# A perceiver layer with experts: the end of the delta-rule stage rewritten to run tile by tile, with the router moved into it

## The reference, cut to what matters

```python
h = rmsnorm(layernorm(x, ln1_g, ln1_b), rms_in_w)
q, k, v = conv_silu(h @ Wq), conv_silu(h @ Wk), conv_silu(h @ Wv)    # 4 heads, keys of 64, values of 128
q, k = l2norm(q) * 64 ** -0.5, l2norm(k)
g, beta = -exp(A_log) * softplus(h @ Wa + dt_bias), sigmoid(h @ Wb)
o = gated_delta_rule(q, k, v, g, beta)                               # a recurrence over the 64 tokens
o = rmsnorm(o, o_norm_w) * silu(h @ Wg)
x1 = xl + o @ Wo
x = x + x1 + gelu(layernorm(x1, ln2_g, ln2_b) @ W2 + b2)
# the experts
n = layernorm(x)
logits = n @ Wr + br                                                 # 8 experts
y = x + softmax(logits)[top] * (gelu(n @ W1[top] + b1[top]) @ W2[top] + b2[top])
```

## Time and profile before

| | us |
|---|---|
| median of 3 runs | 843.79 |
| lowest, highest | 839.43, 844.43 |
| profiled execution, its own time | 846.05 |
| its span in the trace | 844.3 |

### The profile page before, as it was taken

How to read it: one execution, slowest core, us unless ns; L and a number is a source line. 1 busy time by engine, 2 the same in 40 slices (tenths; PEclk the granted TensorE clock), 3 DMA queues, 4 the chain that set the end, 5 groups by cost and what they waited for, 6 DMA issues and landing times. The chain is left out here.

```text
span 844.3 us, 18960 instructions
## 1 busy us (share of the span) xinstructions
PE 684.7 (81%) x7638; PEld 525.9 (62%) x7638; DVE 421.2 (50%) x907; ACT 328.4 (39%) x881; POOL 144.2 (17%) x213
## 2 busy tenths in 40 slices
PE   3778887789899999995787689989986764278996
PEld 2556665565456666663665546579985643178995
DVE  5436787764545445514587275836657344011111
ACT  1235444443445544442577363331224141132332
POOL 1011112201100000003334232091000211211121
PEclk9879998999999999995889699989998965598999
DMA  6920000001900000004000000000000009791110
GB/s 174 357 65 2 2 2 1 1 1 34 230 2 2 1 2 1 2 1 127 2 2 3 1 0 2 2 2 2 0 2 2 0 4 318 274 368 39 46 51 23
DMA packets 33161, 45.30 MB, mean 54 GB/s; under 512 B 7998, under 2 KB 26175, under 8 KB 32960
## 3 DMA queue, kind: packets, MB, share of 16 engines
q1 hardware_dynamic: 28672, 33.31, 12.3%
q0 software_dynamic: 2256, 7.37, 2.7%
q10 hardware_dynamic: 2160, 3.60, 1.6%
HBM read 36.91 MB, written 7.89 MB: 53 GB/s over the span
## 5 line engine op out<-in xcount | busy, mean ns | idle before, releaser
L393 ACT ACTIVATE a_pr<-a_bank,a_nms 128x160 f32<-128x160 f32 x128 | 49.1, 391 | 59.4 <-DVE a_nms L723 57.0
L859 PE MATMUL a_bank<-ident,a_pr 128*80 128x128 f32 x256 | 41.5, 289 | 25.7 <-DVE a_pt L699 23.2
L2101 ACT ACTIVATE f_hb<-f_bank,cols 128x128 f32<-128x128 f32 x96 | 35.2, 367 | 63.1 <-PE f_bank L2219 58.2
L859 PEld LDWEIGHTS a_bank<-ident,a_pr 128*80 128x80 f32 x256 | 26.1, 124 | 46.3 <-ACT a_pr L393 31.8
L2219 PE MATMUL f_bank<-f_xts,f_w 128*128 x384 | 51.6, 293 | 0.8 <-DVE f_xts L2171 0.8
L2219 PEld LDWEIGHTS f_bank<-f_xts,f_w 128*128 128x128 f32 x384 | 50.2, 208 | 1.7 <-issue 1.2
L629 DVE TENSOR_REDUCE a_negmx<-a_bank 128x2 f32<-128x320 f32 x64 | 30.4, 475 | 33.6 <-PE a_bank L851 33.6
L699 DVE COPY a_pt<-a_bank 80x512 f32<-80x512 f32 x60 | 40.9, 682 | 10.5 <-PE a_bank L859 9.8
L2229 PE MATMUL f_bank<-f_w,f_hb 128*128 128x256 f32 x192 | 44.0, 383 | 0.0
L2229 PEld LDWEIGHTS f_bank<-f_w,f_hb 128*128 128x128 f32 x192 | 36.2, 194 | 4.5
L358 POOL TENSOR_TENSOR a_spr<-a_linv,a_hm 128x128 f32<-128x128 f32 x32 | 12.1, 400 | 148.9 <-DVE a_linv L678 136.3
(11 more groups left out here) (361 smaller groups left out, 1607.2 us busy)
## 6 DMA issues: line engine op xcount, KB each, us to landing
f_w<-in_f_w SPq DMA_DIRECT2D x16, 1024.0 KB, 9.8
slots<-a_zero POOLq DMA_DIRECT2D x1, 4112.0 KB, 18.7
f_xs<-slots ACTq DMA_DIRECT2D x13, 257.0 KB, 2.7
a_ct<-in_ctxt SPq DMA_DIRECT2D x15, 160.0 KB, 5.1
rows<-in_rows SPq DMA_DIRECT2D x1, 2120.0 KB, 10.1
x<-in_x SPq DMA_DIRECT2D x2, 512.0 KB, 5.1
b_wq<-in_b_wq SPq DMA_DIRECT2D x1, 1024.0 KB, 6.2
b_wk<-in_b_wk SPq DMA_DIRECT2D x1, 1024.0 KB, 8.3
```

Of the source, the lines that this page charges most:

```text
L393: i = act.activation(pr[:, p, j, k, :], s_bank[j][:, k * KW:(k + 1) * KW], ACT.Exp, bias=nms[:, p, j, k:k + 1], accum_out=rsum[:, p, 2 * j ...
L859: m = pe.transpose(dst[0:HK, (2 * k + a) * P:(2 * k + a + 1) * P], pr[:, p, j, k, a * HK:(a + 1) * HK], c.ident[:, :])
L2101: act.activation(hb[:, m, :], bank[m % 4][:, 0:P], ACT.Gelu, bias=c.col("f_b1", e * FC + m)).then_inc(z["act"], 1)
```

## The change

Where the change stands, in the order of time:

- The values `v` get a tensor of their own, `v0`, that lives through the whole kernel; earlier stages lay two of their tensors into it. In stage E the values are turned ahead of the levels and copied by ScalarE to `bv`; POOL multiplies by beta. When the values have been turned, SyncE loads expert 0 into `v0`.
- The phases after the levels become one loop over t with tiles t, t-1 and t-2 at different steps. Sqrt and reciprocal become Ln and Exp(-0.5 x), in one table set with each other. The Gelu runs four tiles at a time, at t = 5 and t = 9.
- The norm of the experts, its transposes and the router product move into the same loop (`routes`), and the logits are made at the end of stage E. The router's weights and small tables are loaded in stage D.
- Stage F begins with ScalarE's copies of the normed rows and VectorE's maximum of the logits. Eight subtractions become one. It loads experts 1 and 2 at once. The line by which the fourth expert waits for the scatter is unchanged.

The core of the diff, with eight columns of indentation taken off. In the parts of stage E only the new order stands; the removed lines are those of the phases above.

```diff
+    for t, n in ((c.e_wqkv, "e_wqkv"), (c.e_wab, "e_wab"), (c.e_wg, "e_wg"), (c.e_wo, "e_wo"), (c.e_w2, "e_w2"), (c.f_wr, "f_wr")):
+    for t, n in ((c.e_i2, "i2"), (c.e_i2z, "i2z"), (c.e_half, "half"), (c.f_before, "before"), (c.f_ones, "ones"),
+                 (c.f_tab, "f_tab"), (c.f_ids, "f_ids")):
...
+@block.sync
+def _(sp_):
+    sp_.wait_ge(z["vt"], NT)
+    sp_.dma_start(vv[:, 0:2, :], c.d["f_w1"][0, :, :].rearrange("(k p) n -> p k n", p=P)).then_inc(z["expert0"], 16)
+    sp_.dma_start(vv[:, 2:4, :].rearrange("p a (m n) -> p (a m) n", n=D), c.d["f_w2"][0, :, :].rearrange("(k p) n -> p k n", p=P)
+                  ).then_inc(z["expert0"], 16)
+    sp_.wait_ge(z["expert0"], 32)
...
+    for t in range(NT):
+        pool.wait_ge(z["vtc"], t + 1)
+        pool.tensor_tensor(bv[:, t, :, :], bv[:, t, :, :], beta[:, t, :].unsqueeze(2).to_broadcast([P, HG, VD]), ALU.mult
+                           ).then_inc(z["bv"], 1)
...
     act.wait_ge(z["ssq"], 1)
+    act.preload_act_table_set("natural_log_exp_and_others")
     inverse_lengths(0, bank[0][:, 0:32].rearrange("p (t h) -> p t h", h=HG))
+    for t in range(NT):
+        act.wait_ge(z["vt"], t + 1)
+        act.activation(bv[:, t, :, :].rearrange("p h n -> p (h n)"), bank[t], ACT.Copy).then_inc(z["vtc"], 1)
     with act.Fori(1, LEVELS) as lv:
         for g in range(4):
             act.wait_ge(z["y"], 4 * lv + g + 1)
             act.activation(y[:, 8 * g:8 * g + 8, :].rearrange("p a n -> p (a n)"), bank[g], ACT.Copy).then_inc(z["yout"], 1)
     act.wait_ge(z["gw"], NT)
+    for t in range(NT + 2):
+        if t < NT:
+            act.wait_ge(z["dl"], t + 1)
+            act.activation(de[:, t, :, :].rearrange("p h n -> p (h n)"), bank[0], ACT.Copy).then_inc(z["de"], 1)
+        if t > 1:
+            u_ = t - 2
+            act.wait_ge(z["xt2p"], u_ + 1)
+            if u_ > 1:
+                act.wait_ge(z["f2"], u_ - 1)
+            for k in range(KC):
+                a = act.activation(xt2[:, u_ % 2, k, :], bank[5][:, k * P:(k + 1) * P], ACT.Identity,
+                                   scale=c.col("e_g2", k), bias=c.col("e_b2", k))
+            a.then_inc(z["xt2"], 1)
+        if 0 < t <= NT:
+            act.wait_ge(z["ogt"], t)
+            act.activation(de[:, t - 1, :, :].rearrange("p h n -> p (h n)"), bank[3], ACT.Copy).then_inc(z["ogs"], 1)
+        if t < NT:
+            head = slice(HG * t, HG * t + HG)
+            act.wait_ge(z["o"], t + 1)
+            act.activation(bv[:, t, :, :].rearrange("p h n -> p (h n)"), bank[1 + t % 2], ACT.Square).then_inc(z["osq"], 1)
+            act.wait_ge(z["oss2"], t + 1)
+            act.activation(olog[:, head], oss2[:, head], ACT.Ln, scale=1.0 / VD, bias=eps[:, 0:1]).then_inc(z["olog"], 1)
+            act.wait_ge(z["olog"], t + 1)
+            act.activation(orr[:, head], olog[:, head], ACT.Exp, scale=-0.5).then_inc(z["orr"], 1)
+        if 0 < t <= NT:
+            act.wait_ge(z["mv2"], t)
+            act.activation(lrs[:, t - 1:t], w.mv[:, t - 1, 1:2], ACT.Ln, bias=eps[:, 2:3]).then_inc(z["lrs"], 1)
+            act.wait_ge(z["lrs"], t)
+            act.activation(rs2[:, t - 1:t], lrs[:, t - 1:t], ACT.Exp, scale=-0.5).then_inc(z["rs2"], 1)
+        if t in (5, 9):
+            for v in range(t - 5, t - 1):
+                act.wait_ge(z["b2"], v + 1)
+                act.activation(hb[:, v, :], hb[:, v, :], ACT.Gelu).then_inc(z["gel"], 1)
+            act.preload_act_table_set("natural_log_exp_and_others")
+        if t in (6, 9):
+            g = (0, 1)[t > 6]
+            four = slice(4 * g, 4 * g + 4)
+            act.wait_ge(z["mvf"], 4 * g + 4)
+            act.activation(w.ve[:, four], w.mv[:, four, 1], ACT.Ln, bias=eps[:, 2:3]).then_inc(z["lrf"], 1)
+            act.wait_ge(z["lrf"], g + 1)
+            act.activation(w.rs[:, four], w.ve[:, four], ACT.Exp, scale=-0.5).then_inc(z["rsf"], 1)
+        if t in (7, 9):
+            for i in range(2):
+                n = 2 * (0, 1)[t > 7] + i
+                act.wait_ge(z["xtfp"], n + 1)
+                act.activation(xtf[:, i, :, :].rearrange("p k n -> p (k n)"), bank[7], ACT.Copy).then_inc(z["xtf"], 1)
...
+    dve.wait_ge(z["bv"], NT)
+    for t in range(NT + 2):
+        if t < NT:
+            head = slice(HG * t, HG * t + HG)
+            dve.wait_ge(z["osq"], t + 1)
+            dve.reduce_sum(oss[:, head], bv[:, t, :, :], AXX).then_inc(z["oss"], 1)
+            dve.wait_ge(z["oss"], t + 1)
+            dve.tensor_tensor(oss2[:, head], oss[:, head], rq2[:, t, :], ALU.mult).then_inc(z["oss2"], 1)
+        if t > 1:
+            dve.wait_ge(z["f2"], t - 1)
+            dve.tensor_tensor(hb[:, t - 2, :], bank[6][:, 0:D], c.row("e_w2b"), ALU.add).then_inc(z["b2"], 1)
+        if t < NT:
+            dve.wait_ge(z["orr"], t + 1)
+            dve.tensor_tensor(ors[:, head], orr[:, head], rq[:, t, :], ALU.mult).then_inc(z["ors"], 1)
+            dve.wait_ge(z["ors"], t + 1)
+            for hh in range(HG):
+                a = dve.scalar_tensor_tensor(bv[:, t, hh, :], bank[1 + t % 2][:, hh * VD:(hh + 1) * VD],
+                                             ors[:, HG * t + hh:HG * t + hh + 1], gw[:, t, hh, :], ALU.mult, ALU.mult)
+            a.then_inc(z["og"], 1)
+        if 0 < t <= NT:
+            v = t - 1
+            dve.wait_ge(z["enc"], v + 1)
+            dve.tensor_tensor(x1[:, v, :], xl[:, v, :], bank[4][:, 0:D], ALU.add).then_inc(z["x1"], 1)
+            dve.wait_ge(z["x1"], v + 1)
+            dve.bn_stats(w.st[:, v, :], x1[:, v, :]).then_inc(z["stats2"], 1)
+            dve.wait_ge(z["stats2"], v + 1)
+            dve.bn_aggr(w.mv[:, v, :], w.st[:, v, :]).then_inc(z["mv2"], 1)
+            dve.wait_ge(z["mv2"], v + 1)
+            dve.wait_ge(z["rs2"], v + 1)
+            if v > 1:
+                dve.wait_ge(z["xt2p"], v - 1)
+            dve.tensor_scalar(xn2[:, v % 2, :], x1[:, v, :], w.mv[:, v, 0:1], rs2[:, v:v + 1], ALU.subtract, ALU.mult
+                              ).then_inc(z["xn2"], 1)
+        if t in (5, 9):
+            for v in range(t - 5, t - 1):
+                dve.wait_ge(z["gel"], v + 1)
+                dve.wait_ge(z["xs"], v + 1)
+                dve.tensor_tensor(c.x[:, v, :], c.x[:, v, :], hb[:, v, :], ALU.add).then_inc(z["xout"], 1)
+            for v in range(t - 5, t - 1):
+                dve.wait_ge(z["xout"], v + 1)
+                dve.wait_ge(z["xn2"], v + 1)
+                dve.bn_stats(w.st[:, v, :], c.x[:, v, :]).then_inc(z["statsf"], 1)
+            for v in range(t - 5, t - 1):
+                dve.wait_ge(z["statsf"], v + 1)
+                dve.bn_aggr(w.mv[:, v, :], w.st[:, v, :]).then_inc(z["mvf"], 1)
+        if t in (6, 9):
+            g = (0, 1)[t > 6]
+            dve.wait_ge(z["rsf"], g + 1)
+            dve.wait_ge(z["mvf"], 4 * g + 4)
+            for v in range(4 * g, 4 * g + 4):
+                dve.tensor_scalar(c.xn[:, v, :], c.x[:, v, :], w.mv[:, v, 0:1], w.rs[:, v:v + 1], ALU.subtract, ALU.mult
+                                  ).then_inc(z["xnf"], 1)
+    dve.wait_ge(z["logits"], 1)
+    dve.tensor_tensor(c.lg[:, :, :], bank[5][:, 256:320].rearrange("p (t n) -> p t n", n=E),
+                      c.row("f_br").unsqueeze(1).to_broadcast([P, NT, E]), ALU.add).then_inc(z["lg"], 1)
...
+    for t in range(NT):
+        pe.wait_ge(z["gate"], t + 1)
+        if t == 0:
+            pe.wait_ge(z["lss"], 2)
+        for hh in range(HG):
+            a = pe.transpose(bank[t][:, hh * P:(hh + 1) * P], vv[:, hh, t * P:(t + 1) * P], c.ident[:, :])
+        a.then_inc(z["vt"], 1)
+    pe.wait_ge(z["vtc"], 4)
     def product(dst, lhs, rhs, g):
...
             product(bank[g], y, xT, g).then_inc(z["zx"], 1)
+    pe.wait_ge(z["vtc"], NT)
     with pe.Fori(1, LEVELS - 1) as lv:
         level(lv, False)
     level(LEVELS - 1, True)
     pe.wait_ge(z["xt"], 8 * (LEVELS - 1) + 4)
+    def apply(dst, mats, vec, t, done):
         for hh in range(HG):
+            a = pe.matmul(dst[:, hh * VD:(hh + 1) * VD], mats[hh % 2][:, 2 * t + hh // 2, :], vec[:, t, hh, :],
+                          start=True, stop=True)
+        a.then_inc(done, 1)
+    def routes(g):
+        for i in range(2):
+            n = 2 * g + i
+            pe.wait_ge(z["xnf"], 2 * n + 2)
+            if n:
+                pe.wait_ge(z["xtf"], n)
+            for t in (2 * n, 2 * n + 1):
+                for k in range(KC):
+                    at = k * 2 * P + (t % 2) * P
+                    a = pe.transpose(bank[7][:, at:at + P], c.xn[:, t, k * P:(k + 1) * P], c.ident[:, :])
+            a.then_inc(z["xtfp"], 1)
+        for i in range(2):
+            n = 2 * g + i
+            pe.wait_ge(z["xtf"], n + 1)
+            for t in (2 * n, 2 * n + 1):
+                for kk in range(KC):
+                    a = pe.matmul(bank[5][:, 256 + E * t:256 + E * t + E], xtf[:, i, kk, (t % 2) * P:(t % 2 + 1) * P],
+                                  c.f_wr[:, kk, :], start=(kk == 0), stop=(kk == KC - 1))
+        if g:
```

(66 more changed lines are left out.)

228 lines of the change are left out of this document (44 added, 184 removed).

## The result

The changed kernel takes 860.43 us (median of four runs, 854.20 to 862.83), the kernel before 841.84 us on the same chip: a ratio of 1.021 [1.014, 1.028]. The forecast was 858, a ratio of 1.017. The same order of instructions, run again later as e9, gave 858.65 us and 1.019 [1.016, 1.022]. So the change costs about 2%, close to the forecast and mostly for the reason forecast.

The account below looks back on a forecast made before the run. No engine was taken as the bound; the stretch was the sum of its phases. Head 5.0, stream 91.2 for 83.6, boundary 1.3, routing -0.1 gave +13.8: 859.9 us profiled, 858 median, range 846 to 874.

Parts of the forecast that it names:

- a turn closes on itself: Stream loop: TensorE's applies wait behind xn2 of tile t-2, which needs tile t-1's outputs; the chain takes 7.7 us a tile.
- the 91.2: First apply to logits: 84.2 us at TensorE's full clock plus 7 for the clock, in place of 83.6 before.
- The faster rival: Stream: outputs and norm overlap more, the turn falls to TensorE's 5.05 us and TensorE stays warm; -12, 832 us; chance 0.08.
- The clock, +7: Stream: TensorE, idle some 2.6 us a turn, spends a quarter of the time at the lower clock; +7 us, bounds 0 and 26.
- warm: Rival for the stream: TensorE keeps its full clock all through, clock term 0; +6.8, 851 us; chance 0.22.
- cold rival: TensorE at the low clock all through: head 8.5, stream 110; +36, 880 us; chance 0.16, cold or nearly so.
- Head, +5.0: Ahead of the first level: 32 value transposes 3.5 us, table preload 1.3, gap and hand-over 0.2; bounds +3.5 and +8.5.
- Gelu hole +3.5: Sixth turn of the stream: a table load, four Gelu and a load back on ScalarE delay the next apply by 3.5 us.
- Boundary +1.3: Start of stage F, 1.26 us after stage E's last VectorE work, now comes behind the logits; +1.3 us.
- Routing: Logits to positions: seven subtractions fewer save 1.0 us, but VectorE waits for the Exp behind eight ScalarE copies; net -0.1 us.
- First expert and hold, 0: Expert loads: early expert 0 and the fourth expert's unchanged wait for the scatter cost nothing; first expert bounded -2 and +1.
- The drain of a table switch: Three table switches on the new path: by the skill page's drain, an estimated 4 us more, +18 in all.

Follow-up runs that it names:

- e9: Changed kernel once more, its loops written as tables of steps and turns, same instructions in the same order; 858.65 us, 1.019 of the kernel before.
- e2: Changed kernel with the same instructions in a deeper order, each engine's steps spread over five turns in place of two; 831.67 us, 0.987 of the kernel before.
- e5: Changed kernel with four matmuls that feed nothing added behind the first apply of turns 1 to 6; 854.86 us, 1.012 of the kernel before.
- e7: Changed kernel with values of tiles 0 to 3 turned behind the last level, tiles 4 to 7 in turns 0 to 3; 851.25 us, 1.009 of before.
- e1: Kernel before with the change's head alone, the 32 transposes of the values moved ahead of the levels; 845.67 us, 1.0015 of the kernel before.
- e11: Changed kernel with the first expert's loads issued in the last stage in place of during the levels; 864.25 us, 1.024 of the kernel before.
- e10: Changed kernel without the wait on the scatter ahead of the fourth expert's load; 854.74 us, 1.0155 of the kernel before.

## Why the prediction was right, and where it was off

- *The stream sets the loss, because a turn closes on itself.* Right, and shown by removal: 7.4 us a turn at full clock for 7.7, and 5.03 once the chain begins in earlier turns (e2). 90.65 us from the first apply to the end of the logits' bias add, for 91.2.
- *How well the parts of the 91.2 fit.* Less well than the total. The seven terms behind the eighth tile's second apply add up to 27.7, not to 27.3, so the prediction's own sum is +14.2. Measured, that apply starts 60.0 us into the stream (forecast 56.9) and 30.6 us follow. A granted mean of 0.81 over two levels means 38% of the time at the lower one, where the prediction took 25%; the shorter turns made up for it. That is luck.
- *The faster rival, "the circle does not close".* Wrong as the kernel stood, and its number, 832, is what the same instructions give in the deeper order (831.67). That the two agree so closely is partly chance, since 3.8 us of e2's gain lie in D to end. The prediction took the order written in the loop for a fixed cost. It is a choice: the argument against the rival, "every step stands in program order", named the place to change.
- *The clock, +7.* Right in kind. In three profiles of this order the stream took 90.3 to 90.4 us, in a fourth 94.0; full-clock turns take 7.4 and those with a part at half clock 8.3 (655.80 to 664.10). B to C is 3 to 4 us shorter in e5 and in e7, where the clock stays up. The warm and the cold rival both fall: the granted mean of the stream is 0.81.
- *Head, +5.0.* Mis-sized: +6.6. The preload's load was right (1.28). The 32 transposes were costed at the full clock (3.5) and took 5.35, at 0.69 from 561.5 to 567.0; the prediction's own bound for them was 7.0. Against that the levels ran 0.7 faster: the first level's 128 products, which now come behind the transposes, took 3.95 us in place of 5.50, the second's 5.50 in place of 5.22. The head also takes the transposes away from in front of the applies (e1), which the prediction gave no price of its own.
- *Gelu hole +3.5*: 3.17 of idle time. *Boundary +1.3*: 1.34, by the start of stage F at 723.97. *Routing*: from the logits' end to the positions 8.0 us, stage change included, for 8.9 forecast; the eight copies took 2.6 us in place of 3.0, and the running sum started 3.1 us into the stage in place of 3.8. It did start behind the Exp, but only 0.04 of that was the Exp's, the count on TensorE being as late.
- *First expert and hold, 0.* The net was right (130.5 for 130.7 us from the positions to the end) and its reason wrong. The step that failed is "the eight scatters are issued one by one by POOL and paced by it, not by the load". Issue was, landing was not: a scatter landed in 3.3 us (median) before, 6.0 in the changed kernel, 7.7 in e11 and 8.2 in e10. With it fell "end about when the scatter starts, as before". Before, the stage began some 20 us ahead of the positions, and the weights' traffic (380 GB/s) was over 2 us into the scatter; now it begins 7 ahead, and the traffic lasts until 742, past the last scatter's issue at 740.7. The first matmul comes 20.0 us after the positions in place of 18.8. e11, which like the kernel before loads all experts in the last stage, has 134.5 from the positions to the end: so the later start costs some 4 us and the early expert gives some 4 back. Two effects cancelled that the prediction both put at 0; that, too, is luck.
- *The part ahead of A.* 3.5 us of the spans' difference (16.8) was chance, ahead of A (granted clock 0.69 from 450 to 500 us, 0.83 before, 0.84 in e9). Without it the sum over the changed part is +13.3, for +13.8. The medians have more, 18.6 here and 17.4 for e9, for a forecast of 14; the interval of e9's ratio allows 13.5 to 18.5.
- *The drain of a table switch.* The Trainium skill, "ScalarE: Activation LUTs", section What ACT_TABLE_LOAD costs, has about 1.38 us of it at every switch. The trace doesn't agree: the load starts 0.02 us after the last Exp ahead of it (678.28), the first Gelu 0.02 us after its load, and the load back 0.02 us after the last Gelu ends. The price is 1.28 a switch, and the 4 us more that the prediction estimated from the page's figure are not there.

## What to carry to other kernels

When a loop over tiles is software-pipelined on in-order engines, write down the chain from one step of a turn back to the same step of the next: if it runs through steps issued in the same turn, its latency is the turn, whatever the busy shares say, and moving the step that is seen waiting only moves the wait. Spread the chain over more turns until the busiest engine closes the loop; here that took tables of lags, no new instruction and no new buffer, and it won 3%. Put setup work of an engine into that engine's long waits rather than ahead of the phase: in e7 it was free there, and the clock behind the wait stayed up (0.98 in place of 0.58).

## What was not expected of the hardware

Between profiles of code that is the same up to mark A, A lay from 550.7 to 559.5 us: 8.8 us, half of what the change costs by e9's median (17.4). One profile a side doesn't resolve 1% here; stretches inside a profile mostly do, though B to C of the same order was 90.3, 90.4, 90.4 and once 94.0.

A matmul of 128x256 in f32 leaves two records and takes 0.45 us at full clock (eight in 3.62 us), so filler has to be sized from the trace.

The scatter's landing time more than doubled (3.3 to 8.2 us) with the experts' weights in flight beside it (e10: 364 GB/s over that stretch, DMA share 1.06), while its issue on POOL stayed at 0.96 us apiece.
